# A vision tower with experts: the second weighted sum moved past two score tiles, and a root moved from GpSimd to ScalarE

## The chip, the cores and the metric

One Trainium2 chip, one core. The time is the device time of one execution of the whole kernel, in microseconds (us), the median of several runs. Below, TensorE, VectorE, ScalarE, GpSimd and SP are the engines and the queue of SyncE; in rows of a profile they are PE (PEld for its weight loads), DVE, ACT, POOL and SPq.

## The reference

32 images of 224 x 224 are cut into 1024 patches of 49 values each, and pass through three layers, in float32:

```python
h = patches @ W.T + b + pos                       # 32 x 1024 x 64
q, k, v = (h @ Wq.T + bq), (h @ Wk.T + bk), (h @ Wv.T + bv)
mask = (q[:, :, 0] != 0) & (k[:, :, 0] != 0)
prob = softmax(where(mask[:, :, None], q @ k.T / 8, -1e9)); prob = where(mask, prob, 0)
h = layernorm(h + (prob @ v) @ Wo.T + bo)         # over the 64 channels, no gain
x = h.reshape(32768, 64)
probs = softmax(x @ gate_w + gate_b)              # 8 experts
idx = argmax(probs); prb = probs[idx]
pos = running count of idx among the tokens before; kept = pos < 5120
y = (relu(x @ w1[idx] + b1[idx]) @ w2[idx] + b2[idx]) * prb * kept   # 64 -> 256 -> 64
h = layernorm(h + nan_to_num(y))
```

## The kernel before

The program is written by hand for each engine, with semaphores. It runs in steps b = -2 ... 33; step b holds the scores of image b and several other stages beside them:

- the query and key products of image b + 2 (`qk_product`, copied by ScalarE in `qk_copy`, differences of keys by VectorE in `key_steps`, rounded high parts by `k_high` and `qk_high`, low parts by `qk_low`);
- the row maxima of image b + 1 (`max_scores` on TensorE, `row_max` on VectorE, one for each place), later turned and spread by `max_turn` and `shift`;
- the scores of image b in eight places k = 0 ... 7, tiles of 128 keys by 1024 queries (`scores`, six matmuls that add up high and low parts), each followed by an exponential on ScalarE (`exponent`, into one of four buffers `pT[k % 4]`), and the weighted sums over pairs of tiles (`weighted_sum(n, p, r)` for tiles 2r and 2r + 1; `halves` chooses the 512 queries, so that one sum can be issued in two parts);
- for image b - 1 the end of attention: `turn_sums`, `attend` (`tt`), the residual on GpSimd (`uc`), `square` on ScalarE, `sum_squares` on VectorE (`vs`), the root `rstd` = (vs / 64 + eps) ^ -0.5, then `gate_logits`, `gate_gaps`, `gate_choice` on VectorE and `norm_rows` on GpSimd;
- for image b - 2 the position of each token in its expert (`positions`, `slot_read`, `probability`, `slot_index`, which ends with the update of `acc`), and the scatter of its rows into `slots` by GpSimd, one indirect DMA for each of eight tiles;
- from step 6 on, one chunk of 1024 rows of the experts: `load_chunk` on SP (four units of 256 rows, `b_in`, and their experts' weights, `b_w`), `rows_beside`, `rows_turn`, `xT_copy`, `up(c, 0)` and `up(c, 1)` (64 to 256 channels, in two halves), `rectify` after each, `down`, `sums_copy`; one step later `turn_back`, `weigh`, `finite`, `to_numbers`, `residual_sum`, `centre`, `squares`; two steps later `deviation`, `scaled`, `spread_out` (eight indirect DMAs into the output by GpSimd).

After step 33 the remaining chunks run alone (`rounds`). Tables of filled units are made in every second step (b even): `full_units`, `past_experts`, `name_units`.

Each engine runs its own list in program order. The scores have one pair of PSUM banks (`p_st`), so `scores(n, k)` waits for exponential k - 1. The maxima have one pair (`p_sm`), so `max_scores(n, j)` waits for `row_max` j - 1. Both halves of `up` and the projection write `p_misc`, so `up(c, 1)` waits for the four `rectify` of the first half. `exponent(n, k)` waits until the sum that read its buffer is done:

```python
act.wait_ge(st_done, NT * n + k + 1)
after(act, pv_done, 4 * n + k // 2 - 1)
```

For k = 6 this is the sum r = 1. In the chunk steps TensorE's list for places 4 to 7 is: scores 4, maxima 4, up 0, half of sum 1; scores 5, maxima 5, up 1, other half of sum 1; scores 6, maxima 6, projection of image b + 1; scores 7, maxima 7, down, sum 2. On VectorE the row maximum of each place is followed by that place's small work. `to_numbers` comes at place 4, `gate_logits` and `residual_sum` at place 5, `gate_gaps` at place 6, `gate_choice` and `centre` at place 7. The root runs on GpSimd (`norm_root`), between the scatters of image b - 2 and the first `spread_out`.

Of the kernel before, what the change touches and what calls it, by code (L numbers as in the profile page):

```python
# [16 lines left out]
NB = 32  # L17
# [28 lines left out]

UNIT = 256
KHK = 1
HIK = 2
UT = UNIT // P  # L50
# [36 lines left out]
def build(nc, x, posT, wqk, wide, deep, w, out):  # L87
    slots = nc.dram_tensor("slots", (SLOTS, ROW), F32, kind="Internal").ap()
    with ExitStack() as ctx:
# [6 lines left out]
        def sem(name):  # L96
            return ctx.enter_context(nc.semaphore(name))
# [15 lines left out]
        w_t, c_centre, w_v, w_oT, w_g, w_bv, w_bl = views(c_deep, DEEP)  # L113
        c_half = sb("c_half", [P, NT])
        c_neg = sb("c_neg", [P, QT])
# [35 lines left out]
        vs = sb("vs", [P, NT])  # L151
        ve = sb("ve", [P, NT])
        rstd = sb("rstd", [P, NT])
# [182 lines left out]
        pool_step = sem("pool_step")  # L336
        last_sd_ready = sem("last_sd_ready")
        last_rows_ready = sem("last_rows_ready")
# [44 lines left out]

        PS = 2

# [4 lines left out]
        def _(sp):  # L390
# [20 lines left out]
            def load_chunk(c):  # L411
# [17 lines left out]
                for k in range(2 * PAIRS):  # L429
                    v, u = k // 2, k % 2  # L430
                    t = slice(v * UT, (v + 1) * UT)
                    sp.dma_start(b_in[:, r, u, t, :], unit_rows(at[k])).then_inc(c_loaded[r], 16)

                    sp.dma_start(b_w[:, r, v, u, :], w[bass.ds(e[k], 1), :, :].rearrange("a k f -> (a k) f"))\
                        .then_inc(c_loaded[r], 16)
# [47 lines left out]
        def _(pe):  # L483
# [206 lines left out]
            def step(b, c, third, has):  # L690
# [11 lines left out]
                for k in range(NT):  # L702
# [13 lines left out]
                    if back is not None and b <= NB and k == 2:  # L716
                        pe.wait_ge(t_ready, min(b, NB))
                        turn_back(back)
                    if has(1) and (k == 6 or k == 3 and b >= 0):
                        project(b + 1, q, k // 6, has(2))  # L720
# [4 lines left out]
                    if has(0):  # L725
                        if k in (4, 5):
                            weighted_sum(b, par, 1, (k - 4,))
                        if k == 7:
                            weighted_sum(b, par, 2)
# [17 lines left out]
        def _(act):  # L747
# [51 lines left out]

            def last_deviation():  # L800
                act.wait_ge(vs_ready, NB)
                act.activation(sd[:, :], vs[:, :], ACT.Ln, bias=b_eps[:, 0:1], scale=1.0 / D).then_inc(last_sd_ready, 1)
                act.wait_ge(last_sd_ready, 1)
                act.activation(rstd[:, :], sd[:, :], ACT.Exp, scale=-0.5).then_inc(rstd_ready, 1)
# [68 lines left out]
            def step(b, c, third, has):  # L873
# [5 lines left out]
                for k in range(NT):  # L879
                    if k == KHK and has(2):  # L880
                        k_high(b + 2)
                    if k == HIK and has(2):
                        qk_high(b + 2)
                    if k == 1 and has(-1):
# [7 lines left out]
                    if m is not None and k == 2:  # L892
                        xT_copy(m)
                    if k == 5 and b == NB:
                        last_deviation()
                    if m is not None and k in (4, 5):
# [5 lines left out]
                    if k in (3, 6) and has(1):  # L902
                        v_copy(b + 1, q, k // 6)
                if m is not None:
                    sums_copy(m)
# [25 lines left out]
        def _(dve):  # L931
# [47 lines left out]
            dve.memset(ones16[:, :], 1.0)  # L979
            dve.memset(c_half[:, :], -0.5)  # L980
            dve.memset(b_eps[:, :], EPS)
# [251 lines left out]
            def step(b, c, third, has):  # L1233
# [11 lines left out]
                for j in range(NT):  # L1245
# [26 lines left out]
                    if has(-1):  # L1272
# [4 lines left out]
                        if j == 5:  # L1277
                            gate_logits(b - 1)
                        if j == 6:
                            gate_gaps(b - 1)  # L1280
# [4 lines left out]
                    if back is not None:  # L1285
                        if j == 3:
                            finite(back)
                        if j == 4:
                            to_numbers(back)
                        if j == 5:  # L1290
                            residual_sum(back)
                        if j == 7:
                            centre(back)
# [21 lines left out]
        def _(pool):  # L1315
# [23 lines left out]

            def norm_root(n):  # L1340

                wait_apart(pool, vs_ready, n + 1)
                counted(n, 1, pool.tensor_scalar(ve[:, :], vs[:, :], 1.0 / D, EPS, ALU.mult, ALU.add))
                pool.tensor_tensor(rstd[:, :], ve[:, :], c_half[:, :], ALU.pow).then_inc(rstd_ready, 1)

            def norm_rows(n, p):
                pool.wait_ge(rstd_ready, n + 1)
                if n >= 2:
                    pool.wait_ge(scattered[p], of_parity(n - 2, p, 16 * NT))
                pool.tensor_tensor(rows[:, p, :, 0:D], uc[:, :, 0:D], per_token(rstd[:, :], D), ALU.mult)  # L1350
                counted(n, 2, pool.tensor_scalar(rows[:, p, :, D + 1], rows[:, p, :, D + 1], float(2 * S), None,
                                                 ALU.add))

            def scatter(n, p, tiles):
                if 0 in tiles:
# [4 lines left out]
                    else:  # L1360
                        wait_apart(pool, pool_step, PS * n + 2)
                for j in tiles:
# [17 lines left out]
            def step(b, c, third, has):  # L1380
# [4 lines left out]
                if done is not None:  # L1385
# [8 lines left out]
                    scatter(b - 2, par, range(4, NT))  # L1394
                    norm_root(b - 1)
                    spread_out(done, range(5))
# [9 lines left out]
                if has(-1):  # L1406
                    norm_root(b - 1)
                    norm_rows(b - 1, 1 - par)
# [73 lines left out]
```

## Time and profile before

| | |
|---|---|
| median of 3 runs | 1057.18 us (1056.9 to 1058.4) |
| profiled execution, its time | 1059.39 us |
| its span, first to last instruction | 1057.6 us |
| mean granted TensorE clock | 0.952 of full speed |
| TensorE, VectorE, ScalarE, GpSimd busy | 90%, 80%, 66%, 65% of the span |

The busy shares are means over the whole span. The steps with a chunk, 27 of them, take most of it; the last 120 us are the chunks that remain, where GpSimd's scatters and the chunks' own chain set the pace. Times in rows are from the span's start. A matmul's end is modelled, so in the timeline neighbouring matmuls overlap, while the chain of waits gives each its own part of the time.

### The profile page before, as it was taken

Reading aid. Unit: us, or ns where it says so; the run is one execution under the profiler, and the core shown is the slowest. Engines: PE = TensorE matmul, PEld = TensorE weight load, DVE = VectorE, ACT = ScalarE, POOL = GpSimd, SP = SyncE. Lnnn points to the kernel's source line nnn. Section 1 sums busy time; section 2 is a strip of 40 time slices with the busy share of each in tenths; the row PEclk is TensorE's granted clock in tenths of the full one; section 3 lists DMA queues with packets and bytes.
Section 4 is the critical chain, followed back from the end, with each engine's and each line's share of the span. In section 5 each row is a group of like instructions: output and inputs, shape, how many; then the busy total and the mean of one; then the engine's idle time right before and its main releaser. Section 6 shows DMA issues by size and latency. Waiting matters only on the chain.

```text
span 1057.6 us, 19702 instructions
## 1 busy us (share of the span) xinstructions
PE 952.4 (90%) x6046; PEld 530.8 (50%) x6046; DVE 846.5 (80%) x1709; ACT 697.7 (66%) x1192; POOL 691.5 (65%) x689
## 2 busy tenths in 40 slices
PE   3799999999999999999999999999999999856740
PEld 2355545555555555555555555555555555433420
DVE  3667787788888888899989988888889897575561
ACT  2355655777777777777777777777777766545650
POOL 0015444456777777777777777777777777777775
PEclk9699999999999999999999999999999999967775
DMA  3332224334435243334443343424343333035300
GB/s 91 81 77 58 58 59 112 99 85 105 106 79 130 75 110 103 94 96 108 103 107 96 104 109 93 121 68 121 94 104 97 97 93 103 21 106 145 103 22 10
DMA packets 72503, 96.25 MB, mean 91 GB/s; under 512 B 15923, under 2 KB 52230, under 8 KB 72398
## 3 DMA queue, kind: packets, MB, share of 16 engines
q1 hardware_dynamic: 55566, 77.87, 29.7%
q0 software_dynamic: 16832, 17.11, 5.4%
q8 instruction: 49, 0.80, 0.3%
q14 instruction: 56, 0.46, 0.1%
HBM read 43.68 MB, written 18.11 MB: 58 GB/s over the span
## 4 chain that ended last, share of the span: by engine, by line
PE 57%; DVE 23%; ACT 9%; issue 7%; DMA 2%; POOL 1%; SPq 1%; POOLq 0%; DVEq 0%; ACTq 0%
PE p_u L590 14%; DVE mx L1003 8%; PE p_st L568 7%; PE p_misc L605 6%; PE p_misc L513 6%; PE p_misc L669 5%; PE p_misc L536 4%; PE p_sm L550 3%; ACT uu L793 3%; PE p_misc L653 3%; DVE qk L988 2%; ACT qk L759 2%; PE p_st L572 2%; PE p_sm L669 2%; ACT b_h L835 2%
## 5 line engine op out<-in xcount | busy, mean ns | idle before, releaser
L1376 POOL DMA_INDIRECT out<-b_o,b_ix x270 | 295.4, 1094 | 93.4 <-issue 69.3
L1363 POOL DMA_INDIRECT slots<-rows,idx x256 | 252.2, 985 | 146.8 <-issue 87.0
L1003 DVE TENSOR_REDUCE mx<-p_sm 128x1 f32<-128x1024 f32 x252 | 307.1, 1218 | 38.6 <-PE p_sm L552 35.6
L788 ACT ACTIVATE pT<-p_st 128x1024 f32<-128x1024 f32 x256 | 261.8, 1023 | 93.4 <-PE p_st L574 80.5
L590 PE MATMUL p_u<-pT,vv 128*64 128x512 f32 x1024 | 253.7, 605 | 0.0
L568 PE MATMUL p_st<-hi,hx 64*128 64x512 f32 x256 | 127.3, 497 | 5.1 <-ACT pT L788 4.0
L570 PE MATMUL p_st<-hx,hi 64*128 64x512 f32 x256 | 127.3, 497 | 0.0
L590 PEld LDWEIGHTS p_u<-pT,vv 128*64 128x64 f32 x1024 | 61.5, 136 | 105.2 <-issue 94.9
L550 PE MATMUL p_sm<-kh,hi 64*128 64x512 f32 x252 | 103.1, 409 | 10.3 <-DVE mx L1003 6.7
L568 PEld LDWEIGHTS p_st<-hi,hx 64*128 64x128 f32 x256 | 46.9, 183 | 127.3 <-issue 99.7
L835 ACT ACTIVATE b_h<-p_misc,b_w 128x256 f32<-128x256 f32 x244 | 95.6, 475 | 11.5 <-PE p_misc L653 5.2
L552 PE MATMUL p_sm<-kh,hx 64*128 64x512 f32 x252 | 103.0, 409 | 0.0
L568 PE MATMUL p_st<-lo,hx 64*128 64x512 f32 x256 | 100.6, 393 | 0.0
L570 PE MATMUL p_st<-lx,hi 64*128 64x512 f32 x256 | 100.5, 393 | 0.0
L572 PE MATMUL p_st<-hi,lx 64*128 64x512 f32 x256 | 100.2, 392 | 0.0
L574 PE MATMUL p_st<-hx,lo 64*128 64x512 f32 x256 | 100.1, 391 | 0.0
L1333 POOL TENSOR_TENSOR uc<-tt,hh 128x576 f32<-128x576 f32 x31 | 40.8, 1316 | 89.0 <-DVE tt L1030 88.9
L759 ACT ACTIVATE qk<-p_misc 128x1024 f32<-128x1024 f32 x32 | 32.8, 1026 | 72.6 <-PE p_misc L513 71.2
L536 PE MATMUL p_misc<-w_px,xt 114*128 114x137 f32 x504 | 76.6, 296 | 0.0
L846 ACT ACTIVATE b_yT<-p_misc,b_w 64x256 f32<-64x256 f32 x108 | 50.6, 468 | 39.3 <-PE p_misc L669 38.2
L536 PEld LDWEIGHTS p_misc<-w_px,xt 114*128 114x128 f32 x504 | 63.7, 192 | 23.1 <-issue 23.1
L653 PE MATMUL p_misc<-b_xT,b_w 64*128 64x256 f32 x488 | 69.0, 403 | 3.5 <-ACT b_h L835 1.7
(194 smaller groups left out, 1908.5 us busy)
## 6 DMA issues: line engine op xcount, KB each, us to landing
b_w<-in_w SPq DMA_DIRECT2D x136, 193.5 KB
hx<-hi SPq DMA_DIRECT2D x64, 256.0 KB, 3.6
b_in<-slots SPq DMA_DIRECT2D x136, 66.0 KB
lx<-lo SPq DMA_DIRECT2D x32, 256.0 KB
xt<-in_x SPq DMA_DIRECT2D x32, 196.0 KB
out<-b_o,b_ix POOLq DMA_INDIRECT x270
kh<-kh SPq DMA_DIRECT2D x32, 128.0 KB, 2.2
lx<-lo SPq DMA_DIRECT2D x32, 128.0 KB
```

Source lines behind the costliest of these rows:

```text
L536: last = pe.matmul(projected(n, r)[:, j // 2, (j % 2) * GP:(j % 2 + 1) * GP], xt[0:KTOK, n % 3, t * P:(t + 1) * P], w_px[:, :], start=True ...
L550: pe.matmul(max_place(n, j)[:, 0, :], hi[t][0:D, j * P:(j + 1) * P], kh[n % 2][0:D, 0:HALF], start=True, stop=True)
L552: pe.matmul(max_place(n, j)[:, 1, :], hx[t][D:P, j * P:(j + 1) * P], kh[n % 2][D:P, HALF:S], start=True, stop=True).then_inc(sm_done, 1)
L568: pe.matmul(p_st[:, 0, :], hx[t][0:D, kt], upper[t][0:D, 0:HALF], start=first, stop=False, skip_group_check=k > 0)
L570: pe.matmul(p_st[:, 1, :], hi[t][D:P, kt], lower[t][D:P, HALF:S], start=first, stop=False, skip_group_check=k > 0)
L572: pe.matmul(p_st[:, 0, :], lx[t][0:D, kt], hi[t][0:D, 0:HALF], start=False, stop=k > 0, skip_group_check=k > 0)
L590: last = pe.matmul(p_u[c:c + D, a, :], vv[:, p, NT - 1 - k, :], pT[k % 4][:, a * HALF:(a + 1) * HALF], start=(r == 0), stop=(r == 3))
L788: act.activation(pT[k % 4][:, :], flat(p_st), ACT.Exp).then_inc(exp_done, 1)
L835: act.activation(b_h[:, f, u, v, :], place[:, u, v * UNIT:(v + 1) * UNIT], ACT.Relu, bias=b_w[:, r, v, u, W1C + HB * D + f:W1C + HB * D + ...
L1003: dve.tensor_reduce(mx[:, p, at:at + 1], flat(max_place(n, j)), AX.X, ALU.max).then_inc(max_done, 1)
L1363: pool.indirect_dma_start(slots, bass.IndirectOffsetOnAxis(ap=idx[:, p, j:j + 1], axis=0), rows[:, p, j, :], None, bounds_check=SLOTS - 1, ...
L1376: pool.indirect_dma_start(out_rows, bass.IndirectOffsetOnAxis(ap=b_ix[:, o, j:j + 1], axis=0), b_o[:, o, j, :], None, bounds_check=T - 1, ...
```

## The change

1. TensorE: in steps with a chunk, the weighted sum r = 1 is no longer issued in halves behind the up products at places 4 and 5, but whole at place 6, behind the maxima and ahead of the projection. Steps without a chunk keep the halves.
2. VectorE: `to_numbers` moves from place 4 to place 5 (behind `gate_logits`), `residual_sum` from place 5 to place 6 (behind `gate_gaps`, which stays).
3. The root moves from GpSimd (multiply-add and power) to ScalarE (Ln with scale and bias, then Exp with scale -0.5), behind exponential 5 and ahead of the second `rectify`. The last image had it so already.
4. ScalarE's `qk_high` is called at another point of the loop.
5. SP: the loads of a chunk's weights follow its four row loads and each waits for a score tile of the step before the chunk's own (places 4, 5, 6, 7).

```diff
-HIK = 2
+NUJ = 5
+REJ = 6
+GAJ = 6
+NRK = 5
+HIK = 1
...
-        PS = 2
+        PS = 1
...
                     sp.dma_start(b_in[:, r, u, t, :], unit_rows(at[k])).then_inc(c_loaded[r], 16)
-
+                for k in range(2 * PAIRS):
+                    v, u = k // 2, k % 2
+                    if c < INSIDE:
+
+                        sp.wait_ge(st_done, NT * (HOST[c] - 1) + NT // 2 + 1 + k)
                     sp.dma_start(b_w[:, r, v, u, :], w[bass.ds(e[k], 1), :, :].rearrange("a k f -> (a k) f"))\
                         .then_inc(c_loaded[r], 16)
...
+                    if k == 6 and m is not None and has(0):
+                        weighted_sum(b, par, 1)
                     if has(1) and (k == 6 or k == 3 and b >= 0):
                         project(b + 1, q, k // 6, has(2))
...
-                        if k in (4, 5):
+                        if k in (4, 5) and m is None:
                             weighted_sum(b, par, 1, (k - 4,))
...
-            def last_deviation():
-                act.wait_ge(vs_ready, NB)
-                act.activation(sd[:, :], vs[:, :], ACT.Ln, bias=b_eps[:, 0:1], scale=1.0 / D).then_inc(last_sd_ready, 1)
-                act.wait_ge(last_sd_ready, 1)
+            def norm_root(n):
+                act.wait_ge(vs_ready, n + 1)
+                if n >= 1:
+                    act.wait_ge(tail_g, GS * (n - 1) + 1)
+                    act.wait_ge(pool_step, n)
+                act.activation(sd[:, :], vs[:, :], ACT.Ln, bias=b_eps[:, 0:1], scale=1.0 / D).then_inc(sd_ready, 1)
+                act.wait_ge(sd_ready, n + 1)
                 act.activation(rstd[:, :], sd[:, :], ACT.Exp, scale=-0.5).then_inc(rstd_ready, 1)
...
-                    if k == HIK and has(2):
-                        qk_high(b + 2)
...
-                    if k == 5 and b == NB:
-                        last_deviation()
+                    if k == NRK and has(-1):
+                        norm_root(b - 1)
...
+                    if k == HIK and has(2):
+                        qk_high(b + 2)
...
-                        if j == 4:
+                        if j == NUJ:
                             to_numbers(back)
-                        if j == 5:
+                        if j == REJ:
                             residual_sum(back)
...
-            def norm_root(n):
-
-                wait_apart(pool, vs_ready, n + 1)
-                counted(n, 1, pool.tensor_scalar(ve[:, :], vs[:, :], 1.0 / D, EPS, ALU.mult, ALU.add))
-                pool.tensor_tensor(rstd[:, :], ve[:, :], c_half[:, :], ALU.pow).then_inc(rstd_ready, 1)
-
...
-                    norm_root(b - 1)
                     spread_out(done, range(5))
                     norm_rows(b - 1, 1 - par)
```

## Rows read from the trace of the kernel before

**Rows 1.** The page, busy us, share of the span and instructions of each engine.
```profile
PE 952.4 (90%) x6046; PEld 530.8 (50%) x6046; DVE 846.5 (80%) x1709; ACT 697.7 (66%) x1192; POOL 691.5 (65%) x689
```

**Rows 2.** Two neighbouring steps as stretches, from `key_steps` to `key_steps`.
```profile
core 0: us, PE busy (x) PEld busy (x) DVE busy (x) ACT busy (x) POOL busy (x), PEclk, DMA share, GB/s
498.27:526.57 28.30, 28.23 (x189) 15.97 (x187) 25.67 (x49) 21.28 (x36) 21.28 (x21) 1.00 0.40 102
469.60:498.27 28.67, 28.28 (x187) 15.88 (x185) 25.69 (x55) 21.28 (x37) 21.65 (x21) 1.00 0.40 101
```

**Rows 3.** Chain of waits, odd step: start, us on the chain, engine, tile, line.
```profile
504.65 1.87 PE p_u L590 x8
...
509.79 0.43 PE p_st L568
...
510.92 0.91 PE p_misc L653 x7
511.82 1.01 PE p_u L590 x4
...
513.96 0.86 PE p_misc L653 x8
...
516.96 1.13 PE p_misc L536 x8
...
518.99 0.46 PE p_sm L550
```

**Rows 4.** Chain of waits, the even step before it.
```profile
483.30 1.13 DVE mx L1003
...
489.48 1.14 DVE mx L1003
...
490.66 0.50 PE p_sm L550
```

**Rows 5.** ScalarE in the odd step (timeline), and one stretch: Ln and Exp of `deviation`.
```profile
502.78 1.06 ACT L771 ACTIVATE hi<-qk 128x1024 fp32r<-128x1024 f32 x1
503.72 0.30 ACT L868 ACTIVATE b_sd<-b_vs,b_eps 128x8 f32<-128x8 f32 x1
...
510.73 1.03 ACT L788 ACTIVATE pT<-p_st 128x1024 f32<-128x1024 f32 x1
511.89 1.57 ACT L835 ACTIVATE b_h<-p_misc,b_w 128x256 f32<-128x256 f32 x4
...
503.72:504.27 0.55, 0.55 (x8) 0.41 (x6) 0.45 (x4) 0.51 (x3) 0.00 (x0) 1.00 0.21 62
```

**Rows 6.** VectorE, odd step; then stretches: `to_numbers`, gate to `acc` (odd, even).
```profile
511.50 1.21 DVE L1003 TENSOR_REDUCE mx<-p_sm 128x1 f32<-128x1024 f32 x1
...
526.57 1.09 DVE L988 TENSOR_TENSOR qk<-qk,p_misc 64x896 f32<-64x896 f32 x1 [0.52 <-ACT qk L759]
...
512.63:514.43 1.80, 1.80 (x16) 1.43 (x16) 1.73 (x4) 1.49 (x4) 1.60 (x2) 1.00 0.79 220
515.56:526.06 10.50, 10.50 (x73) 5.76 (x73) 9.72 (x27) 7.03 (x15) 8.10 (x9) 1.00 0.22 51
487.27:497.57 10.30, 9.96 (x67) 5.38 (x69) 9.55 (x26) 6.48 (x14) 7.90 (x9) 1.00 0.51 127
```

**Rows 7.** Step 31: stretch of GpSimd's root, timeline of `acc` and the scatter.
```profile
907.43:910.06 2.63, 2.63 (x20) 1.29 (x18) 1.77 (x4) 2.35 (x5) 2.35 (x2) 1.00 0.04 13
...
920.04 0.16 DVE L1177 TENSOR_TENSOR acc<-acc,ohs 128x8 bf16<-128x8 bf16 x1
...
922.34 0.97 POOL L1363 DMA_INDIRECT slots<-rows,idx  x1 [0.30 <-issue]
```

**Rows 8.** ScalarE's first use of a chunk (timeline); DMA issues of the page.
```profile
529.66 0.62 ACT L817 ACTIVATE b_x<-b_in 128x512 f32<-128x512 f32 x1
...
hx<-hi SPq DMA_DIRECT2D x64, 256.0 KB, 3.6
```

**Rows 9.** All `t_x` of the trace (min/median/max ns), and a `uc` (timeline).
```profile
L1154 DVE TENSOR_TENSOR t_x<-t_m x15: 166/1306/1310, 168.1 to 928.7; 128x8 f32<-128x8 f32 x15
...
505.04 1.31 POOL L1333 TENSOR_TENSOR uc<-tt,hh 128x576 f32<-128x576 f32 x1 [1.67 <-DVE tt L1030]
```

More of the change, by code:

```diff
@@ L113, in build @@
         w_t, c_centre, w_v, w_oT, w_g, w_bv, w_bl = views(c_deep, DEEP)
-        c_half = sb("c_half", [P, NT])
         c_neg = sb("c_neg", [P, QT])
@@ L151, in build @@
         vs = sb("vs", [P, NT])
-        ve = sb("ve", [P, NT])
         rstd = sb("rstd", [P, NT])
@@ L336, in build @@
         pool_step = sem("pool_step")
-        last_sd_ready = sem("last_sd_ready")
+        sd_ready = sem("sd_ready")
         last_rows_ready = sem("last_rows_ready")
@@ L979, in _ @@
             dve.memset(ones16[:, :], 1.0)
-            dve.memset(c_half[:, :], -0.5)
             dve.memset(b_eps[:, :], EPS)
@@ L1278, in step @@
                             gate_logits(b - 1)
-                        if j == 6:
+                        if j == GAJ:
                             gate_gaps(b - 1)
@@ L1350, in norm_rows @@
                 pool.tensor_tensor(rows[:, p, :, 0:D], uc[:, :, 0:D], per_token(rstd[:, :], D), ALU.mult)
-                counted(n, 2, pool.tensor_scalar(rows[:, p, :, D + 1], rows[:, p, :, D + 1], float(2 * S), None,
+                counted(n, 1, pool.tensor_scalar(rows[:, p, :, D + 1], rows[:, p, :, D + 1], float(2 * S), None,
                                                  ALU.add))
@@ L1360, in scatter @@
                     else:
-                        wait_apart(pool, pool_step, PS * n + 2)
+                        wait_apart(pool, pool_step, PS * n + 1)
                 for j in tiles:
@@ L1406, in step @@
                 if has(-1):
-                    norm_root(b - 1)
                     norm_rows(b - 1, 1 - par)
```

## The prediction

> **What bounds the kernel now.** I read four views. The page first [rows 1]: TensorE is busy 90% of the span and VectorE 80%; with a nearly full TensorE, a moved instruction pays only if it closes a gap. Then the stretches of two neighbouring steps [rows 2]. The subtraction of `key_steps` starts at 469.60, 498.27 and 526.57: a step whose image is even lasts 28.67 us (its VectorE also makes a table of units), an odd one 28.30, both at the full clock (1.00, so 2.4 GHz), with TensorE busy 28.2 of them and VectorE 25.7. I call them table steps and plain steps.
>
> Then the chain of waits. In the plain step [rows 3] it stays on TensorE from the scores of place 4 (509.79) to the down products (519.45 = 518.99 + 0.46): scores and maxima 1.13 a place, up products 0.91 and 0.86, each half of the weighted sum 1.01, the projection 1.13. In the table step [rows 4] the same stretch belongs to VectorE: a row maximum, `to_numbers`, the gate, `residual_sum`, and the maximum of place 6, whose end at 490.62 releases `max_scores` at 490.66; the down products follow at 491.16. So plain steps are TensorE's, table steps VectorE's, but by a hair: 28.67 against 28.30.
>
> Last the timelines of ScalarE, VectorE and GpSimd [rows 5 to 7], to see what each has to spare. VectorE idles 0.52 before `key_steps` in the plain step, where it waits for ScalarE's `qk`.
>
> **What costs nothing.** `HIK = 1` with the later position in the loop body leaves `qk_high` between the exponential of place 1 and `deviation`: the same order as now. The loads of `b_w` come after all four of `b_in` and wait for places 4 to 7 of the step before their use. The last would be issued when the scores of place 7 end, near 520 in the plain step; ScalarE first needs the chunk for `b_x` at 529.66, and a transfer of 256 KB takes 3.6 us from issue to landing [rows 8], so some 6 us are left. Behind the waits in SP's queue stands `spread_low`, which waits for VectorE's `lo` of the next step and is not held up. In steps without a chunk only the root moves: 0.
>
> **The plain step, from place 4.** The last TensorE number before any change is 510.92 (509.79 + 1.13).
> - Up products 0 end at 511.82. The first half of the sum, which stood here, is gone, so the scores of place 5 come 1.01 earlier: exponential 4 ends at 511.76 [rows 5], just in time. Scores take 0.90 of the 1.13, maxima 0.23: 512.72.
> - `max_scores` 5 waits for row maximum 4, which ends at 512.71 [rows 6]. Its start after a wait costs 0.50, as at 490.66 [rows 4]: 513.24.
> - Up products 1 need all four `rectify` of the first half, which read the banks that they write. These run 511.89 to 513.46 [rows 5] and can't start before exponential 4 has ended. So 513.50, and 0.86 + 0.09 for a fresh start: 514.45.
> - Exponential 5 is queued on ScalarE behind those `rectify`: 513.46 to 514.48. Scores 6 wait for it: 514.52, 0.95 after a wait, maxima 0.23: 515.70.
> - The whole second sum takes 1.87, as the whole first one does [rows 3], where two halves took 2.02: 517.57. Projection 1.13: 518.70. Exponential 6 has to wait for this sum (it overwrites `pT[2]`), runs 517.6 to 518.6, and hides exactly behind the projection. Without the projection it would cost 1.0.
> - Scores 7 and maxima: 519.83, against 519.45 now. Part of the stalls is paid back: 0.15 by the halves, and 0.23 since `max_scores` 7 no longer starts after a wait.
>
> TensorE's path is thus 0.4 longer. VectorE's: the root now comes from ScalarE after exponential 5; Ln and Exp take 0.55, as the pair of `deviation` does [rows 5]: 515.03. VectorE, done with row maximum 5 by 514.4, has idled 0.6 there. From `gate_logits` to the end of the update of `acc` it now needs 10.50 (515.56 to 526.06) [rows 6]; `to_numbers`, moved behind the gate, adds 1.80. In the 10.50 lies an idling of 0.27 before `shift`, which goes: the ends and durations of VectorE's rows there leave that much open. 515.05 + 10.50 - 0.27 + 1.80 = 527.08, against 526.57, where `key_steps` starts now. So 0.5 by VectorE, 0.4 by TensorE and ScalarE. I take 0.45; the bounds are 0.3 (should ScalarE's next instruction begin 0.1 before its predecessor ends, as 503.72 does before 503.84 [rows 5], at two places) and 0.6 (a fresh start as dear as that of `max_scores` 5, 0.23 more).
>
> **The table step.** Row maximum 4 ends at 484.43 [rows 4], so maxima 5 run 484.47 to 484.97, and up products 1 to 485.83. The `rectify` four, at the same place in the step as in the plain one, end at 484.81; exponential 5 at 485.83; scores and maxima 6 at 487.0; sum and projection 490.0; scores and maxima 7 491.1, against 491.16. VectorE: root at 486.38; the path from `gate_logits` is 10.30 - 0.27 + 1.80 and ends at 498.2, where `key_steps` starts now at 498.27 [rows 2, 6]. The relief that the moved `residual_sum` brings to maximum 7 is given back by the wait for the root and by TensorE's stalls. I take -0.05, bounds -0.3 and +0.2.
>
> **The root's other half, GpSimd.** `ve` and the power go from its queue: 907.43 to 910.06, 2.63 [rows 7]. In a steady step GpSimd waits for `tt` anyway. In step 31 it doesn't: from there it has no wait until the last scatters, which release the loads of the last chunks. But the scatter of image 30, at 922.34, also needs `acc`, ready at 920.20 [rows 7]; and step 31 has no projection behind which to hide exponential 6, so its TensorE is some 0.8 later (1.0 less the 0.15 of the halves). 921.1 instead of 922.3: -1.2. Bounds: 0 and -2.6.
>
> **Sum.** Full steps with a chunk and maxima are 6 to 30: 12 plain, 13 table. 12 x 0.45 - 13 x 0.05 - 1.2 = 3.6 us. The profiled execution took 1059.39 around a span of 1057.6, 2.2 above the median of 1057.18; 3.6 is added to the median: **1060.8**. From the bounds: 12 x 0.3 - 13 x 0.3 - 2.6 = -2.9, and 12 x 0.6 + 13 x 0.2 + 0 = 9.8.
>
> One row speaks against moving work on GpSimd. `t_x` takes 1.31 in the median but 0.17 at the least [rows 9]; the long ones start with GpSimd's `uc`, the addition that also follows `tt` [rows 9]: so the one holds the other for up to 1.14. With the root gone, the multiplication of `norm_rows` starts some 2.3 earlier, beside row maximum 6, and ends where the gate's subtraction is due. Met badly, it would hold VectorE for up to 1.1 in each of 25 steps, 27 us. The Trainium skill, "SBUF — State Buffer", section "Who interferes with whom", says that a VectorE instruction with two SBUF inputs contends with a GpSimd instruction that reads SBUF, and one of them fully blocks. By that rule the trace agrees for `t_x`, and a row maximum, which reads PSUM, would not be held.
>
> **The rivals.**
> - *Faster.* The moved `residual_sum` shortens the chain that now sets the table steps. If row maximum 4 and the first `rectify` did not hold TensorE, a plain step would run from 510.92 through 0.90 + 1.13 + 0.86 + 1.13 + 1.87 + 1.13 + 1.13 to 519.07, 0.38 early, and the table step, whose place 4 lies 28.66 ahead, to 490.4, 0.76 early: 13 x 0.76 + 12 x 0.38 + 2.6 = 17.0, so 1040. For it: 1.35 less in front of maximum 7 (28.67 against 28.30 shows that VectorE's chain counts). Against: the `rectify` four take 1.57, and the chain exponential 4, `rectify`, exponential 5, root is pure ScalarE time. It decides from where a plain step costs less than 0.1; half of it, about 1049, is the more likely form. 0.22.
> - *No change.* The plain step costs only 0.1 to 0.25, as ScalarE's overlaps and VectorE's 0.79 of idling (0.27 and 0.52) take up the rest: 12 x 0.2 - 0.65 - 1.2 = 0.5, so 1057.7. 0.28.
> - *Ports*, as above: 1088, or 1074 if every second step is hit. That a row maximum (1.21 beside GpSimd's power as without it) isn't stretched speaks against it. 0.05.
> - *Late weights.* If the last load landed after 529.66, every microsecond would count 26 times, 1087 for one. The 6 us of margin speak against it. 0.03.
> - *My sum*, 1059.3 to 1067: 0.42.
>
> **How the numbers follow.** 0.2% is 2.1 us, about what a measurement of this kernel can tell from no change. Slower is my sum and the last two rivals, 0.50; same 0.28; faster 0.22. The likeliest case is 1060.8, its own range 1059.3 to 1067. For 8 in 10 I leave out the far half of the faster case, ports and late weights: 1051 to 1068.
>
> **What would show it.** Right: in plain steps a gap on TensorE before up products 1, which begin when the `rectify` end; VectorE waiting 0.3 to 0.7 for `rstd` from ScalarE before `lg`; no wait before `key_steps`; plain steps at 28.7 and table steps at 28.6; GpSimd waiting for VectorE before the scatter of image 30. Wrong: steps below 28.3, exponential 6 ending after the projection, or `b_x` waiting for a DMA. The prediction fails most easily at the plain step's 0.45, a difference of two long paths, each made of six or more rows.

## The result and the profile after

The changed kernel takes 1068.18 us (median of 4 runs, 1067.74 to 1068.84), the kernel before 1057.79 on the same chip: a ratio of 1.0098, with an interval of 1.0085 to 1.0111. It is 10.4 us slower. The forecast was slower, 3.6 us, in a range that ended at 1068. In a later comparison the changed kernel took 1066.61 against 1057.66 (1.0081, 1.0062 to 1.0100). The profiled execution took 1067.95 around a span of 1066.2, the one before 1059.39 around 1057.6: 8.56 more, and by these two executions the difference is split up below.

The page, engines, after (compare [rows 1]):

```profile
PE 954.5 (90%) x6046; PEld 530.9 (50%) x6046; DVE 859.2 (81%) x1708; ACT 706.0 (66%) x1254; POOL 618.0 (58%) x627
```

GpSimd lost 73 us of work and ScalarE gained 8. VectorE executed one instruction less (the constant for GpSimd's root is no longer written) and was busy 12.7 us longer: some of its instructions have become longer, and that is the first thing to look for.

The same two steps as stretches, from `key_steps` to `key_steps` (compare [rows 2]: 28.67 and 28.30); the even one, a table step, first:

```profile
core 0: us, PE busy (x) PEld busy (x) DVE busy (x) ACT busy (x) POOL busy (x), PEclk, DMA share, GB/s
474.08:503.06 28.98, 28.48 (x189) 16.08 (x189) 26.33 (x55) 21.80 (x39) 19.27 (x19) 1.00 0.36 96
503.06:531.79 28.73, 28.11 (x187) 15.80 (x185) 25.69 (x49) 21.25 (x39) 18.67 (x19) 1.00 0.40 104
```

These table steps differ by 0.31, these plain steps by 0.43. VectorE is busy 26.33 in the table step and was 25.69 before.

The chain of waits in the plain step, after (compare [rows 3]):

```profile
515.71 0.93 PE p_misc L659 x8
...
517.76 0.49 ACT b_h L846
...
518.30 1.14 PE p_misc L659 x8
...
520.40 1.90 PE p_u L596 x8
...
522.38 1.03 ACT pT L796
...
524.65 1.88 PE p_misc L675 x16
```

Between the two up products stand now only the scores of place 5, and the chain passes through the last `rectify` (`b_h`); the whole sum is followed by ScalarE's exponential 6, as long as the projection that runs beside it.

VectorE in the table step and then in the plain step, after (timeline: start, us, operation, idle time before it and who ended it):

```profile
490.65 0.22 DVE L1070 TENSOR_TENSOR lg<-uc,rstd 128x64 f32<-128x64 f32 x1
...
493.24 1.21 DVE L1013 TENSOR_REDUCE mx<-p_sm 128x1 f32<-128x1024 f32 x1
494.36 0.96 DVE L1079 TENSOR_TENSOR ld<-lb,lm 128x64 f32<-128x64 f32 x1
...
502.86 0.16 DVE L1187 TENSOR_TENSOR acc<-acc,ohs 128x8 bf16<-128x8 bf16 x1
503.06 1.09 DVE L998 TENSOR_TENSOR qk<-qk,p_misc 64x896 f32<-64x896 f32 x1
...
519.62 0.23 DVE L1070 TENSOR_TENSOR lg<-uc,rstd 128x64 f32<-128x64 f32 x1 [0.30 <-ACT rstd L815]
...
523.34 0.35 DVE L1079 TENSOR_TENSOR ld<-lb,lm 128x64 f32<-128x64 f32 x1
...
531.79 1.09 DVE L998 TENSOR_TENSOR qk<-qk,p_misc 64x896 f32<-64x896 f32 x1 [0.20 <-ACT qk L767]
```

GpSimd at the same two places:

```profile
494.15 1.08 POOL L1354 TENSOR_TENSOR rows<-uc,rstd 128x512 f32<-128x512 f32 x1
...
522.52 1.08 POOL L1354 TENSOR_TENSOR rows<-uc,rstd 128x512 f32<-128x512 f32 x1
```

In the table step `norm_rows` runs from 494.15 to 495.23. VectorE's gate subtraction `ld` becomes due at 494.36, in the middle of it, and ends at 495.32 instead of after its usual 0.21. In the plain step `ld` is due at 523.34, and only the last 0.26 of `norm_rows` lies over it. The row maximum ahead of it, which reads PSUM and ends under the same `norm_rows`, has its 1.21 as ever. The chain of waits of the table step runs through the held `ld`, and from there on VectorE alone to the next `key_steps`:

```profile
494.44 0.89 DVE ld L1079
...
502.86 0.17 DVE acc L1187
```

All `ld` of the trace, after and then before (min/median/max ns):

```profile
L1079 DVE TENSOR_TENSOR ld<-lb,lm x32: 208/350/965, 82.8 to 945.1; 128x64 f32<-128x64 f32 x32
```

```profile
L1069 DVE TENSOR_TENSOR ld<-lb,lm x32: 212/215/218, 83.0 to 934.3; 128x64 f32<-128x64 f32 x32
```

In the steps without a chunk it is another small instruction, the addition behind the gate's product (VectorE, then GpSimd):

```profile
176.53 0.95 DVE L1072 TENSOR_TENSOR lb<-lg,c_wide 128x64 f32<-128x64 f32 x1
```

```profile
176.32 1.08 POOL L1354 TENSOR_TENSOR rows<-uc,rstd 128x512 f32<-128x512 f32 x1 [2.96 <-ACT rstd L815]
```

**Where the 8.56 lie.** By the starts of `key_steps` in both traces. 11 stretches of plain steps, 0.43 each: +4.7. 11 of table steps, 0.32 each in the mean: +3.5. The first long stretch, which before had 27.95 and after has 28.75 like the others: +0.80. Five stretches without a chunk, 23.74 in place of 23.55 and the like: +0.96. Everything ahead of them: -0.79. From the last `key_steps` (840.09 before, 849.29 after) to the end of the span, with one more plain and one more table step in it: 216.9 in place of 217.5, -0.6.

### The profile page after: what moved, and what is told of

Same layout as the page of the kernel before. It is cut to its first block, busy times and chain, and to the rows that moved or that the text cites. A ratio compares the mean times of both kernels' runs of the same rounds, so it can differ in the third digit from the quotient of the medians.

```text
span 1066.2 us, 19733 instructions
## 1 busy us (share of the span) xinstructions
PE 954.5 (90%) x6046; PEld 530.9 (50%) x6046; DVE 859.2 (81%) x1708; ACT 706.0 (66%) x1254; POOL 618.0 (58%) x627
## 4 chain that ended last, share of the span: by engine, by line
PE 50%; DVE 27%; ACT 11%; issue 8%; DMA 2%; POOL 1%; SPq 1%; POOLq 0%; ACTq 0%; DVEq 0%
PE p_u L596 13%; DVE mx L1013 8%; PE p_st L574 7%; PE p_misc L611 6%; PE p_misc L519 4%; PE p_misc L659 3%; PE p_misc L675 3%; ACT b_h L846 3%; PE p_sm L556 3%; ACT uu L801 3%; PE p_misc L542 3%; DVE qk L998 2%; PE p_st L578 2%; PE p_sm L675 2%; ACT pT L796 2%
## 5 line engine op out<-in xcount | busy, mean ns | idle before, releaser
L1380 POOL DMA_INDIRECT out<-b_o,b_ix x270 | 283.7, 1051 | 95.9 <-issue 75.0
L596 PE MATMUL p_u<-pT,vv 128*64 128x512 f32 x1024 | 247.9, 603 | 0.0
L596 PEld LDWEIGHTS p_u<-pT,vv 128*64 128x64 f32 x1024 | 63.8, 136 | 111.5 <-issue 107.5
L659 PE MATMUL p_misc<-b_xT,b_w 64*128 64x256 f32 x488 | 71.9, 414 | 7.0 <-ACT b_h L846 5.0
```

Of the source, the lines that this page charges most:

```text
L596: last = pe.matmul(p_u[c:c + D, a, :], vv[:, p, NT - 1 - k, :], pT[k % 4][:, a * HALF:(a + 1) * HALF], start=(r == 0), stop=(r == 3))
L1380: pool.indirect_dma_start(out_rows, bass.IndirectOffsetOnAxis(ap=b_ix[:, o, j:j + 1], axis=0), b_o[:, o, j, :], None, bounds_check=T - 1, ...
```

## The experiments

Two theories after the first look. **A**: TensorE's order is what costs, above all the whole sum with exponential 6 behind it. **B**: the sum's place is neutral or useful, and what costs is VectorE's new order with the root; after the first four runs GpSimd's `norm_rows` at a bad place was added to it. "before + ..." is the kernel before with one part of the change, "after - ..." the changed kernel without one.

### The parts one by one

**halves_back**: after, with the second sum in halves again.

```diff
-                    if k == 6 and m is not None and has(0):
-                        weighted_sum(b, par, 1)
-                        if k in (4, 5) and m is None:
+                        if k in (4, 5):
```

> The changed kernel with one part undone: the weighted sum r = 1 again in halves behind the up products at places 4 and 5. VectorE's order, the root on ScalarE and the later weight loads stay. Theory A (the moved sum is what costs, through the stalls before up products 1 and scores 6): plain steps go back to 28.3 and table steps to 28.6, 1058 to 1060 in all. Theory B (VectorE is the bound and its new order leaves it without work between row maxima 4 and 5, whoever issues the sum where): TensorE then brings maxima 5 one microsecond later, VectorE's path from the gate to key_steps is 1.8 us longer than before and starts about 0.3 us earlier at best, so plain steps stay at 28.7 to 29.0 and the time at 1066 to 1072.

1088.77 (1.0292, 1.0271 to 1.0313): 20 us *slower* than the changed kernel, where theory A had it near the time before. Theory A, as an account of the whole loss, falls. Table steps now last 28.66 as a rule, plain steps 30.28 and 31.60 in turn. VectorE and then GpSimd in a long one:

```profile
528.70 1.89 DVE L1210 COPY_PREDICATED b_n<-b_fin,b_p 128x512 f32<-128x512 uint8 x1
```

```profile
528.93 1.06 POOL L1352 TENSOR_TENSOR rows<-uc,rstd 128x512 f32<-128x512 f32 x1
```

The predicated copy takes 1.89 instead of 0.73, beside `norm_rows`, in nearly every plain step (12 of 34 copies are held). The step of 28.66 has no such hold and is as long as the table step of rows_at7 (28.70, below), which has the whole sum: there the sum's place makes no difference. In plain steps it shifts VectorE against GpSimd. The further 1.3 of every second plain step are waits of VectorE for the turned maxima (0.74) and of `key_steps` for ScalarE (0.52); what brings them was not traced. A plain step with the sum in halves, the root on ScalarE and no hold was not run, so what the sum's place alone costs there stays open.

**sum_alone**: before + the whole second sum at place 6.

```diff
+                    if k == 6 and m is not None and has(0):
+                        weighted_sum(b, par, 1)
-                        if k in (4, 5):
+                        if k in (4, 5) and m is None:
```

> The kernel before with one part of the change: the weighted sum r = 1 whole at place 6 in chunk steps. Theory A (the stalls of TensorE cost 0.4 a step whatever VectorE does): 1067 to 1069. Theory B (with to_numbers still in front of row maximum 5, that maximum ends at 515.6 in the plain step of before, maxima 6 wait for it, and the sum and the projection stand behind them; 0.85 us a step): both kinds of step near 29.2 to 29.5, about 1078.

1081.25 (1.0220, 1.0199 to 1.0241), steps of 29.68 and 29.34. The chain of waits in a step shows why:

```profile
522.45 0.34 DVE b_neg L1199
...
522.82 0.70 DVE b_n L1202
...
523.54 0.74 DVE b_n L1204
524.28 1.11 DVE mx L1005
...
525.44 0.50 PE p_sm L550
525.94 1.89 PE p_u L590 x8
...
527.91 1.03 ACT pT L790
```

With the first half of the sum gone, the maxima come a microsecond earlier, but row maximum 5 still stands behind `to_numbers`. Maxima 6 wait for it, the sum behind them, and exponential 6 behind the sum.

**order_alone**: before + `to_numbers` at place 5 and `residual_sum` at place 6.

```diff
-                        if j == 4:
+                        if j == 5:
                             to_numbers(back)
-                        if j == 5:
+                        if j == 6:
                             residual_sum(back)
```

> The kernel before with one part of the change: to_numbers at place 5, residual_sum at place 6 on VectorE. Root on GpSimd, halves at places 4 and 5. Theory A (a mere reordering in VectorE's list is free or a gain, since residual_sum no longer delays maxima 7): 1050 to 1058. Theory B (VectorE idles before row maximum 5 and pays for it at key_steps): plain steps 28.8 to 28.9, table steps 28.7 to 28.8, 1063 to 1067.

1091.36 (1.0312, 1.0291 to 1.0333), steps of 29.81 and 29.99: far above what either theory said. VectorE, then GpSimd:

```profile
526.36 1.23 DVE L1003 TENSOR_REDUCE mx<-p_sm 128x1 f32<-128x1024 f32 x1 [1.31 <-PE p_sm L552]
...
531.98 1.94 DVE L1207 TENSOR_TENSOR b_u<-b_n,b_in 128x512 f32<-128x512 f32 x1
```

```profile
532.30 1.06 POOL L1350 TENSOR_TENSOR rows<-uc,rstd 128x512 f32<-128x512 f32 x1
533.43 0.60 POOL L1351 TENSOR_SCALAR rows<-rows 128x8 f32<-128x8 f32 x1
```

`b_u`, the core of `residual_sum`, takes 1.94 in the place of 0.69: `norm_rows` again, now beside an instruction on 128x512 elements with two inputs from SBUF. VectorE also idles 1.31 before row maximum 5, a gap that `to_numbers` used to fill.

**root_alone**: before + the root on ScalarE (with `HIK = 1`), GpSimd's root removed.

```diff
-HIK = 2
+HIK = 1
...
+                    if k == NRK and has(-1):
+                        norm_root(b - 1)
...
-                    norm_root(b - 1)
                     spread_out(done, range(5))
```

> The kernel before with one part of the change: the root on ScalarE behind exponential 5. Theory A (the root's 0.55 us on ScalarE and VectorE's wait for it are a cost in every step): plain steps above 28.5, 1062 or more. Theory B (it is hidden, as the gate comes at 515.56 and the root would be ready at 515.3): plain steps 28.3 to 28.4, steps without a chunk 0.2 longer each as in the changed kernel, the tail shorter by up to 2; 1055 to 1059. Table steps tell of the ports: norm_rows then ends beside the gate's subtraction; if that takes 0.5 or more instead of 0.21, table steps are longer by as much.

1058.12 (0.9999, 0.9985 to 1.0012), steps of 28.64 and 28.30. In steps with a chunk the root's move costs and brings nothing by itself; in the five steps without one it has the 0.2 of the changed kernel (23.73, 23.71). Its `ld`, which the expectation set as the test of the ports, takes 0.28 to 0.30: `norm_rows` starts 0.86 before it, so that only the last 0.2 lie over it.

### norm_rows at another place

**rows_at7**: after, with seven row groups of `spread_out` in front of `norm_rows` instead of five, which puts it 2.57 us later on GpSimd (22.64 after `key_steps` in the table step, not 20.07).

```diff
-                    spread_out(done, range(5))
+                    spread_out(done, range(7))
                     norm_rows(b - 1, 1 - par)
-                    spread_out(done, range(5, NT))
+                    spread_out(done, range(7, NT))
```

> The changed kernel, with GpSimd's norm_rows behind seven of the eight spread_out issues instead of five: it begins near 496.7 in the table step and 525.0 in the plain one, beside the sum b_mu and row maximum 7, which read one tensor. Theory P (norm_rows holds VectorE's gate subtraction ld, 0.96 instead of 0.21 in table steps, 0.35 in plain ones, and 0.33 of it reaches key_steps in table steps): ld at 0.21 everywhere, table steps 28.6 to 28.7, plain steps 28.7 as now, 1062 to 1065. Rival (ld is long for another reason, such as the exponentials or the loads of the weights now landing there): ld stays at 0.6 in the mean and the time at 1067 to 1069.

1064.23 against 1058.48 (1.0055, 1.0036 to 1.0075). The two steps, and all its `ld`:

```profile
472.16:500.86 28.70, 28.20 (x187) 15.93 (x185) 25.64 (x54) 21.52 (x38) 19.80 (x19) 1.00 0.37 99
500.86:529.63 28.77, 28.40 (x189) 15.99 (x187) 25.65 (x50) 21.52 (x38) 18.61 (x19) 1.00 0.40 102
```

```profile
L1079 DVE TENSOR_TENSOR ld<-lb,lm x32: 208/214/221, 82.2 to 941.3; 128x64 f32<-128x64 f32 x32
```

There it lies beside row maximum 7, in the plain step also beside `b_mu`, a reduction with one input. No `ld` is held, the table step is back at 28.70 (28.62 by the forecast), and VectorE is busy 25.64 in it, not 26.33. The plain step stays at 28.77, so its length was never the ports'. Both kinds of step now end with `key_steps` waiting for ScalarE's copy `qk`, which itself waits for TensorE's product: with the hold gone, TensorE's side sets the pace and VectorE has 0.3 to 0.4 to spare:

```profile
529.63 1.09 DVE L998 TENSOR_TENSOR qk<-qk,p_misc 64x896 f32<-64x896 f32 x1 [0.36 <-ACT qk L767]
```

**rows_at6**: the same with six groups, so 1.29 us later than after.

```diff
-                    spread_out(done, range(5))
+                    spread_out(done, range(6))
...
-                    spread_out(done, range(5, NT))
+                    spread_out(done, range(6, NT))
```

> The changed kernel with norm_rows behind six spread_out issues: it begins 0.3 after VectorE's residual addition b_u (two operands from SBUF), as in the kernel with the new order alone, where b_u took 1.94 instead of 0.71. Theory P: b_u takes 1.9 in most steps, both kinds of step 0.5 to 1.0 longer than in the changed kernel, 1078 to 1092, although the engine that is moved has nothing on the path. Rival (GpSimd's place doesn't matter): 1067 to 1069.

1087.67 (1.0276, 1.0249 to 1.0303): 23 us between six and seven groups. Steps last 29.47 and 29.81. In table steps `norm_rows` misses `ld` and meets `b_u` (1.94, 11 of the 34 `b_u` are held); in plain steps it still holds `ld`, and for longer than in the changed kernel (1.6, 12 of 32). The expectation, `b_u` at 1.9 in most steps, was right in time and only half right in place. All `ld` and all `b_u` of the trace, then VectorE and GpSimd in a plain step:

```profile
L1079 DVE TENSOR_TENSOR ld<-lb,lm x32: 207/216/1635, 83.2 to 963.7; 128x64 f32<-128x64 f32 x32
...
L1217 DVE TENSOR_TENSOR b_u<-b_n,b_in x34: 691/693/1945, 236.1 to 1056.2; 128x512 f32<-128x512 f32 x34
...
530.62 1.64 DVE L1079 TENSOR_TENSOR ld<-lb,lm 128x64 f32<-128x64 f32 x1
...
531.08 1.08 POOL L1354 TENSOR_TENSOR rows<-uc,rstd 128x512 f32<-128x512 f32 x1
```

**order_rows_at6**: the two edits of order_alone and of rows_at6 together, on the kernel before.

> The kernel with VectorE's new order alone (1091.4), and norm_rows behind six spread_out issues, beside row maximum 7. Theory P (1.23 of the 1.5 us that the order costs in every step is the hold of b_u by norm_rows, the rest the gap before row maximum 5): b_u back to 0.7, steps near 28.7, 1059 to 1065. Rival (the order itself costs 1.3 a step, by VectorE's gap before row maximum 5): 1085 or more.

1063.87 (1.0052, 1.0035 to 1.0070), steps of 28.67 and 28.79. All `b_u`, order_alone and then order_rows_at6:

```profile
L1207 DVE TENSOR_TENSOR b_u<-b_n,b_in x34: 691/1936/1953, 233.8 to 1062.8; 128x512 f32<-128x512 f32 x34
```

```profile
L1207 DVE TENSOR_TENSOR b_u<-b_n,b_in x34: 691/691/694, 233.1 to 1034.6; 128x512 f32<-128x512 f32 x34
```

So 27.5 of the 33 us of order_alone came from the place of `norm_rows`; 5.4 are the order itself. Its plain step is as long as the changed kernel's although the sum is in halves and the root on GpSimd. It ends in another way: `key_steps` waits for nothing, so VectorE's list sets the length here:

```profile
528.30 1.09 DVE L988 TENSOR_TENSOR qk<-qk,p_misc 64x896 f32<-64x896 f32 x1
```

### The useful half

**residual_alone**: before + `residual_sum` at place 6; `to_numbers` stays at place 4.

```diff
-                        if j == 5:
+                        if j == 6:
                             residual_sum(back)
```

> The kernel before with residual_sum alone at place 6; to_numbers stays at place 4 and fills VectorE's gap there. Root on GpSimd, halves at 4 and 5, norm_rows at 519.9 of the plain step. Theory Q (of the reordering only this half was of use: it releases maxima 7 of the table step 1.35 earlier, and VectorE has 0.8 of idling in the plain step to take it up): table steps 28.1 to 28.3, plain steps 28.2 to 28.4, 1049 to 1054. Rival (VectorE's path from row maximum 6 to key_steps, longer by 1.35, eats the gain, or b_u meets norm_rows): 1057 or more.

1048.90 (0.9906, 0.9882 to 0.9929); once more, as residual_again, 1047.28 (0.9911, 0.9890 to 0.9932). It beats both kernels. One table and one plain step of it:

```profile
466.80:494.95 28.15, 28.11 (x187) 15.93 (x185) 25.58 (x54) 21.35 (x37) 21.10 (x20) 1.00 0.38 100
494.95:523.05 28.10, 27.98 (x189) 15.94 (x187) 25.45 (x49) 21.21 (x36) 21.74 (x22) 1.00 0.40 106
```

This table step is 0.52 shorter than before and one of the longer ones; most last 28.06 to 28.08, 0.6 shorter. TensorE is busy 28.11 of its 28.15, and `key_steps`, which in the kernel before waited for `qk` at the end of every step with a chunk, no longer does: VectorE's list now ends last. VectorE in it:

```profile
485.61 1.23 DVE L1003 TENSOR_REDUCE mx<-p_sm 128x1 f32<-128x1024 f32 x1 [0.40 <-PE p_sm L552]
...
487.69 0.69 DVE L1207 TENSOR_TENSOR b_u<-b_n,b_in 128x512 f32<-128x512 f32 x1 [0.21 <-DVE pm L1075]
```

Row maximum 6 no longer has `b_u` and `b_mu` in front of it and waits for TensorE, 0.40, where before TensorE waited for it [rows 4].

> The kernel before with residual_sum alone at place 6, again, beside the one with the root moved: 1047 to 1051 on an undisturbed chip, ratio 0.99 to the kernel before; on a disturbing one within 2% of the kernel before.

**residual_root_third**: residual_alone with the root on ScalarE, as in root_alone, and `norm_rows` behind seven groups.

```diff
+                    if k == NRK and has(-1):
+                        norm_root(b - 1)
...
-                        if j == 5:
+                        if j == 6:
                             residual_sum(back)
...
-                    norm_root(b - 1)
-                    spread_out(done, range(5))
+                    spread_out(done, range(7))
```

> residual_sum alone at place 6, root on ScalarE, norm_rows behind seven issues. On a chip where the kernel before takes some 1058: 1046 to 1049 by theory P, 1050 or more by its rival (the root's 0.55 on ScalarE counts). Should the kernel before take 1130 again, the comparison with the other three of this call tells whether such a chip hits kernels with the root on ScalarE more than others.

1049.96 (0.9925, 0.9908 to 0.9942), steps of 28.18 and 28.26: nothing more than residual_alone.

**loads_back_third**: after, with the four loads of `b_w` issued where they were.

```diff
-                for k in range(2 * PAIRS):
-                    v, u = k // 2, k % 2
-                    if c < INSIDE:
-                        sp.wait_ge(st_done, NT * (HOST[c] - 1) + NT // 2 + 1 + k)
```

> The changed kernel without its waits for score tiles in front of the weight loads: 1067 to 1069 if the loads are hidden in both places. On a chip that disturbs: beside the changed kernel itself in this call; the same within 1% if the loads' place does not matter.

1067.39 (1.0094, 1.0077 to 1.0111), beside 1066.61 for **changed_again**, the changed kernel itself:

> The changed kernel itself, on the chip of this call: 1067 to 1069 on an undisturbed chip. Theory: its ratio to the kernel before is 1.01 as before; on a disturbing chip it tells whether the long waits come with the root on ScalarE (then 1.15 or more) or not.

The later loads cost nothing and bring nothing that can be measured.

The kernels of residual_root_third and of loads_back_third had each been run twice before, in two comparisons in which the kernel before itself took 1133.04 and 1131.66 us, 7% more than elsewhere: **residual_root_at7** took 1359.50 and **residual_root_again** 1354.45, **loads_back** 1322.51 and **loads_back_again** 1324.01, at a mean granted clock of 0.86 to 0.87. What was expected, in the same order:

> The kernel with residual_sum alone at place 6 (1048.9), and the root on ScalarE with norm_rows behind seven spread_out issues, so that it stands where GpSimd's root left it. Theory P (GpSimd's place relative to VectorE decides, the root itself is free): steps as in that kernel, ld and b_u at 0.2 and 0.7, the tail 1 to 2 shorter, 1046 to 1049. Rival (the root costs ScalarE 0.55 that now counts, as plain steps have less slack): 1050 or more.

> The same kernel as residual_root_at7 (residual_sum alone at place 6, root on ScalarE, norm_rows behind seven issues), again, since in the first try the kernel before itself took 1133 on that chip and every engine waited long for things outside the program. Expected as there: 1046 to 1049 by theory P, 1050 or more by its rival.

> The changed kernel with the loads of the weights issued as before, each behind its rows and with no wait for score tiles. Theory: they are hidden in both places, 1067 to 1069. Rival (the late loads cost or gain something, through waits of b_x or traffic beside the scatters): beyond 1065 to 1071, and b_x would wait for a DMA in the changed kernel.

> The same kernel as loads_back (the changed kernel with the weight loads issued as before), again for the same reason. Expected as there: 1067 to 1069 if the loads are hidden in both places, beyond 1065 to 1071 by the rival.

Differences of 1% can't be read from these four, and they decide nothing. The first of the two comparisons was on the chip on which the kernel before had taken 1058.48 beside rows_at7, so the chip is not always so slow. What slowed everything there, and these kernels more than the one before, stays open.

## Why the forecast was right in direction and too small

**The plain step was right in size, and in mechanism on TensorE's and ScalarE's side.** Counted from `key_steps`, forecast and measured: up products 1 begin at 15.23 and 15.24; the whole sum at 17.43 and 17.34; exponential 6 at 19.33 and 19.32; the down products at 21.56 and 21.59; `lg` after the root at 16.78 and 16.56; the next `key_steps` at 28.81 (by VectorE's path) and 28.73. 0.45 was said, 0.43 came. TensorE stalls for the `rectify`, exponential 6 just hides behind the projection, and VectorE waits for `rstd`: 0.30, where the forecast had 0.6. Which path ends last came out otherwise. VectorE's update of `acc` ends at 28.53, not 28.81, and `key_steps` waits 0.20 for `qk`, where "no wait before `key_steps`" was to be the sign: the 0.43 is the forecast's 0.4 of TensorE and ScalarE, and not its 0.5 of VectorE. rows_at7, 28.77 with no `ld` held, shows that this length does not come from GpSimd's hold.

**The step that failed is the table step's -0.05; it costs 0.31.** The chain up to the down products was right there too (21.53 after `key_steps`, 21.5 by the forecast). `lg` came 0.21 earlier than forecast, at 16.57. From `lg` to the end of `acc` the forecast had 11.83 (10.30 - 0.27 + 1.80), the trace has 12.37: the gate subtraction alone gained 0.75 over its 0.21, other instructions gave 0.2 back. That is the rival *Ports*, at the place where it was put ("ends where the gate's subtraction is due"), but with another size: not 1.1 in each of 25 steps, but 0.75 in table steps and 0.14 in plain ones. Of the 0.75, about 0.3 reaches `key_steps`, which otherwise would have waited 0.44 for `qk`: rows_at7, which moves `norm_rows` and nothing else, has table steps of 28.70 to the changed kernel's 28.98, and is 1.0055 of the time before where the changed kernel is 1.0098. Its chance, 0.05, was too low. What spoke against it was true, that a row maximum is not held, but the small instruction behind the maximum is. The forecast weighed the maximum against the ports and not what VectorE runs right after it.

**The sum by its terms.** Forecast 3.6, measured 8.56 between the two profiled executions:
- table stretches: 3.5 + 11 x 0.05, +4.0 over the forecast, and the first long stretch, counted as a table step, +0.85
- steps without a chunk: forecast "only the root moves: 0", measured 0.96. The root's move starts `norm_rows` 0.8 later there (176.32, before 175.51) and lets it meet `lb`, which takes 0.95 instead of 0.23; before, it met `lg` (0.45 instead of 0.23). root_alone has these steps at 23.73 too, and order_rows_at6, with GpSimd's root, at 23.54
- plain stretches: 4.7 against 11 x 0.45, -0.2
- ahead of the fourth `key_steps`, where nothing was forecast: -0.79. Two runs of one kernel, residual_alone and residual_again, differ by 2.4 there, so I put it to no cause
- the end: -0.6 against 0.45 - 0.05 - 1.2 = -0.8, +0.2.

3.6 + 4.0 + 0.85 + 0.96 - 0.2 - 0.79 + 0.2 = 8.6. The medians differ by 10.4, as the profiled execution of before was one of the longer ones (1059.39 with a median of 1057.79).

**The tail's -1.2 came out as a sum and not by its route.** GpSimd's last scatters, after (compare [rows 7]):

```profile
931.84 0.98 POOL L1367 DMA_INDIRECT slots<-rows,idx  x1 [1.87 <-issue]
933.99 0.97 POOL L1367 DMA_INDIRECT slots<-rows,idx  x1 [1.17 <-issue]
```

GpSimd stands idle for 1.87 before the first of them, where before it had 0.30, so it does wait, as forecast; the row doesn't name for what. But the scatter of image 30 is 0.3 later relative to the steps (9.50, of them 9.20 from the steps), not 1.2 earlier. In step 31 `acc` is 25.91 after the one of step 30, where it was 25.09: the 0.8 by which TensorE was to be later (order_rows_at6, with the sum in halves, has 25.10). But the scatter starts 0.85 after `acc` ends, not 0.1. The end of the kernel nevertheless came back to -0.6; which of the last loads and products does that I have not tested.

**Late weights**: as forecast, nothing; loads_back_third shows it. The only waits of `b_x` for a load are two of the tail's, 3.3 us together; before there were three, 4.5.

**Faster**: its mechanism, that the moved `residual_sum` shortens the chain of the table steps, is real: residual_alone takes 6.4 off the eleven table stretches and 2.8 off the eleven plain ones, 9.2 together, and 9.6 and 10.4 us by medians. In the changed kernel nothing of it is left. By the chains this is what the forecast put against it, the chain of `rectify`, exponential 5 and root, and `to_numbers` on VectorE's path; no run takes these two apart.

**Why the parts don't add.** Alone, the sum costs 23.0 us, the order 33.1, the root and the loads nothing; together they cost 10.4. The sum at place 6 needs `to_numbers` out of the way of row maximum 5, which the order does. The order alone lands `norm_rows` on `b_u`; with the early maxima and the root on ScalarE, it lands on the smaller `ld`. halves_back, order and root without the sum, lands it on the predicated copy in plain steps.

## What to carry to other kernels

When an edit shifts GpSimd's queue, list what VectorE runs at each new place of GpSimd's tensor instructions, down to the small ones: place them beside row maxima that read PSUM, and try the neighbouring places. An instruction off the critical path moved by 1.3 us changed this kernel by 23 us. Time the parts of a change alone as well as together: here the sum of the parts was 56 us, the whole 10, and one part by itself was the improvement that the whole did not give.

## What the runs showed of the hardware

**Of two neighbours one waits for the other, and the recorded starts don't tell which.** In order_alone `b_u` began at 531.98 and `norm_rows` at 532.30; `b_u` took 1.94 in place of 0.69, and ended 0.56 after `norm_rows`, as if it had done next to nothing until then. In halves_back the predicated copy began at 528.70, 0.23 before `norm_rows` at 528.93, and took 1.89 in place of 0.73. In rows_at6 `ld` began at 530.62 and would have been over at 530.83, 0.25 before `norm_rows` began at 531.08; it took 1.64 and ended 0.10 after it. But in one step of the kernel before, VectorE's `b_n` began 0.11 ahead and kept its 0.69, and `norm_rows` took 1.48 in place of 1.06:

```profile
227.54 0.69 DVE L1200 TENSOR_TENSOR b_n<-b_pos,b_neg 128x512 f32<-128x512 f32 x1
227.65 1.48 POOL L1350 TENSOR_TENSOR rows<-uc,rstd 128x512 f32<-128x512 f32 x1
```

The Trainium skill, "SBUF — State Buffer", section "SBUF: two separate sides", says that of a VectorE instruction with two inputs from SBUF and a GpSimd one the first to start gets the shared ports for its whole length, and the other fully blocks. That one of them fully blocks agrees with these rows. That it is the later one agrees with the last pair and not with the three before it, if the recorded starts are the moments at which the ports are taken; whether they are, no run here shows. GpSimd's next instruction, on 128x8 elements, took 0.60 beside the held `b_u` and 0.25 beside the small `ld`, so it seems to have been held a little in turn.

**A small instruction can wait for the whole rest of GpSimd's.** `ld` and `lb`, with 64 elements a partition, went from 0.21 and 0.23 to 0.96 and 0.95 in the changed kernel, up to 0.09 after the end of GpSimd's multiplication, and `ld` to 1.64 in rows_at6. Row maxima, which read PSUM, kept 1.20 to 1.23 in the kernel before, in the changed one and in all the experiments that ran at the usual speed.
